# Attention into routed experts on one core: turned rows kept in DRAM, expert weights in pieces, and a written-out order for the last units' routing

## What is computed

```python
x = x + xattn(ctx, layernorm(x), mask)            # 64 x 128 tokens, 256 wide; 4 heads of 64
h = layernorm(x)
s = sigmoid(h @ router.T); f = s + router_bias    # 32 experts in 4 groups
# the 2 best groups by the sum of their 2 best f; then the 4 best experts of these
w = 2.5 * s[chosen] / sum(s[chosen])
y = sum_k w[k] * down[e_k] @ (silu(gate[e_k] @ h) * (up[e_k] @ h))
x = x + y + sdown @ (silu(sgate @ h) * (sup @ h)) # a shared expert, for every token
```

## Time and profile before

| | |
|---|---|
| median of three runs | 1495.28 us (1495.05 to 1497.76) |
| the profiled execution, its own time | 1499.18 us |
| its span, first to last instruction | 1497.4 us |
| mean granted TensorE clock | 0.978 of full speed |
| busy: PE, PEld, DVE, ACT, POOL | 90%, 70%, 64%, 71%, 41% |
| DMA | 241.80 MB, mean 161 GB/s |

### The profile page before, as it was taken

How to read it: one execution, slowest core, us unless ns; L and a number is a source line. 1 busy time by engine, 2 the same in 40 slices (tenths; PEclk the granted TensorE clock), 3 DMA queues, 4 the chain that set the end, 5 groups by cost and what they waited for, 6 DMA issues and landing times.

```text
span 1497.4 us, 33141 instructions
## 1 busy us (share of the span) xinstructions
PE 1347.0 (90%) x8742; PEld 1045.2 (70%) x8742; DVE 965.8 (64%) x4500; ACT 1057.4 (71%) x2886; POOL 610.7 (41%) x662
## 2 busy tenths in 40 slices
PE   3999999999999999997568888988988988889997
PEld 1566666666666666665457877877887887878886
DVE  3468888888888888887473444444444444437777
ACT  3899999999999999996534555555555555553432
POOL 1003444444544445445433555554555555540000
PEclk9899999999999999999699999999999999999999
DMA  7323454445444544443646444544544444419786
GB/s 227 123 81 137 175 175 141 153 173 174 153 144 168 177 174 136 157 149 132 190 134 228 139 142 144 144 141 133 145 141 139 146 143 138 115 42 341 275 287 206
DMA packets 145252, 241.80 MB, mean 161 GB/s; under 512 B 23467, under 2 KB 109357, under 8 KB 143792
## 3 DMA queue, kind: packets, MB, share of 16 engines
q1 hardware_dynamic: 118960, 172.27, 36.3%
q0 software_dynamic: 26112, 67.42, 12.6%
HBM read 102.20 MB, written 118.00 MB: 147 GB/s over the span
## 4 chain that ended last, share of the span: by engine, by line
PE 44%; ACT 34%; issue 10%; DVE 5%; another core or an unknown queue 3%; DMA 2%; POOL 1%; SPq 1%; ACTq 0%; DVEq 0%; POOLq 0%
PE psT L900 9%; PE psS L910 9%; PE ps L900 8%; ACT arena L1028 7%; ACT arena L1036 5%; PE ps L891 4%; PE ps L832 3%; ACT arena L1044 3%; PE psT L832 3%; ACT arena L996 2%; ACT arena L1000 2%; ACT arena L956 2%; PE psS L841 2%; ACT arena L988 1%
## 5 line engine op out<-in xcount | busy, mean ns | idle before, releaser
L588 POOL DMA_INDIRECT expert_out<-pay,dest x288 | 283.7, 985 | 269.5 <-DVE pay L1657 107.6
L533 POOL DMA_INDIRECT lists<-pay,slot x168 | 171.8, 1022 | 221.6 <-issue 49.2
L910 PE MATMUL psS<-arena,history 128*128 x576 | 182.2, 398 | 59.3 <-DVE history L1650 42.6
L1657 DVE TENSOR_SCALAR pay<-psS,dest 128x256 f32<-128x256 f32 x288 | 138.7, 481 | 77.3 <-PE psS L910 73.5
L900 PEld LDWEIGHTS ps<-pad 128*128 128x128 f32 x1152 | 149.5, 192 | 17.0 <-ACT pad L1196 7.9
L900 PEld LDWEIGHTS psT<-pad,hist_j 128*128 128x128 f32 x1152 | 150.4, 193 | 12.6 <-issue 2.2
L900 PE MATMUL ps<-pad 128*128 128x128 f32 x1152 | 154.0, 277 | 4.1 <-ACT pad L1196 2.6
L900 PE MATMUL psT<-pad,hist_j 128*128 128x128 f32 x1152 | 154.3, 277 | 0.9 <-ACT pad L1196 0.9
L910 PEld LDWEIGHTS psS<-arena,history 128*128 128x128 f32 x576 | 87.4, 192 | 76.7 <-issue 75.6
L533 POOL DMA_INDIRECT lists<-arena,slot x88 | 90.0, 1022 | 106.6 <-PE psT L711 19.7
L641 PE MATMUL ps<-arena 128*128 128x512 f32 x256 | 129.8, 630 | 1.9 <-ACT arena L988 1.7
(11 more groups left out here) (233 smaller groups left out, 3348.5 us busy)
## 6 DMA issues: line engine op xcount, KB each, us to landing
lists<-pad SPq DMA_DIRECT2D x72, 516.0 KB, 7.8
pay<-lists SPq DMA_DIRECT2D x288, 129.0 KB
arena<-expert_out SPq DMA_DIRECT2D x32, 1024.0 KB, 6.1
pay<-pay SPq DMA_DIRECT2D x40, 384.0 KB
x<-in_x SPq DMA_DIRECT2D x32, 256.0 KB
out<-arena SPq DMA_DIRECT2D x32, 256.0 KB, 4.9
arena<-arena SPq DMA_DIRECT2D x20, 384.0 KB
arena<-in_ctx SPq DMA_DIRECT2D x32, 192.0 KB
```

Source lines behind the costliest of these rows:

```text
L533: pool.indirect_dma_start(lists, bass.IndirectOffsetOnAxis(ap=slots(u)[:, j, k:k + 1], axis=0), paid(u)[:, j, k, :], None).then_inc(scat[u ...
L588: pool.indirect_dma_start(expert_out, bass.IndirectOffsetOnAxis(ap=dest[:, t % DESTS, 1:2], axis=0), yy[n], None, bounds_check=T * TOPK - ...
L910: pe.matmul(dbank[n % 2][:, 0:D], hh[:, n % 4, :], w_dn[:, at(e, 1), :].rearrange("p a n -> p (a n)"), start=True, stop=True)\
L1657: dve.tensor_scalar(yy[n], dbank[n % 2][:, 0:D], dest[:, t % DESTS, 0:1].bitcast(fp32), None, ALU.mult)\
```

## The change

A DRAM tensor `n1T_kept` takes the turned rows of units 0 to 7 while attention runs, and they are read back in step 31 into room that the last projections left. `EARLY` is 8. These eight units have no `norm_again`, no `shared_turn` and no `turned`; unit 0's `shared_up` stands inside attention's last step. Up's PSUM banks alternate by unit. Gate and up weights come from one DRAM tensor, in six DMAs: experts 0 to 5 and 14 to 16 after the last `turn_q`, 17 to 31 after the last output, then 6 to 8, 9 to 11 and 12 to 13 as the shared units have read their rows. Down weights 0 to 19 wait for the scatters of unit 28. Unit 30's copies are made by SP; unit 31's three copies by ACT, after its one row. Routing of units 29 to 31 is moved forward on PE, ACT and DVE and interleaved. The experts' two places for copied weights are swapped (not shown).

```diff
 EARLY = 7 -> 8;  IN_ARENA removed
+    n1T_kept = nc.dram_tensor("n1T_kept", [EARLY, P, 2 * D], fp32).ap()
+        early_n1T = arena[:, first_n1T * 2 * D:above * 2 * D].rearrange("p (u n) -> p u n", u=EARLY)
+        up_banks = [[ps[2], ps[0]], [ps[3], ps[1]]]
...
 SyncE
+            def save_n1T(u):
+                sp.wait_ge(e_n, u.n + 1)
+                sp.dma_start(n1T_kept[u.n], n1T.rearrange("p k n -> p (k n)")).then_inc(n1T_saved, 16)
+            def load_n1T():
+                sp.wait_ge(n1T_saved, 16 * EARLY)
+                sp.wait_ge(hats, UNITS)
+                sp.wait_ge(pb_full, NB)
+                sp.wait_ge(pc_full, NB)
+                sp.wait_ge(ss_done, NB)
+                for u in range(EARLY):
+                    sp.dma_start(early_n1T[:, u], n1T_kept[u]).then_inc(n1T_in[u], 16)
             def step(s):
                 if (s + 3).exists():
                     load(s + 3)
+                if s.n == UNITS - 1:
+                    load_n1T()
+                if (s + -2).exists():
+                    spread_rows(s + -2)
                 if s.exists():
                     blank_unit(s)
-                if (s + -2).exists() and s.exists():
-                    spread_rows(s + -2)
+                if (s + -2).exists() and s.n - 2 < EARLY:
+                    save_n1T(s + -2)
...
+            sp.wait_ge(t_q, UNITS)
+            load_experts(0, first_n1T)
+            load_experts(above, below_wo)
+            spread_rows(Unit(UNITS // 2 - 1, 0))
             sp.wait_ge(y_done, NB)
-            for k in range(2):
-                for which, w in ((0, gate), (1, up)):
-                    sp.dma_start(w_gu[:, :, k, which * I:(which + 1) * I], w[:, k]).then_inc(weights_e, 16)
-            sp.wait_ge(sx_done, 2 * IN_ARENA)
+            load_experts(below_wo, E)
+            sp.wait_ge(scat[1], scattered(1, UNITS - 1))
             sp.dma_start(w_dn[:, 0:early], down[:, 0:early]).then_inc(weights_e, 16)
+            for lo, hi in ((0, 3), (3, 6), (6, EARLY)):
+                sp.wait_ge(sgu_full, 2 * hi)
+                load_experts(first_n1T + lo, first_n1T + hi)
...
 TensorE, in step 31
                 if cc.exists():
                     logits(cc)
+                if not a.exists():
+                    shared_up(0, 0)
+                    shared_up(0, 1)
...
                 mix_values(s, 1)
+                else:
+                    positions(s + -2)
                 out_proj(s, 1)
...
 TensorE, behind it
+            turn_n1(last + -1)
+            shared_up(1, 0)
+            logits(last + -1)
+            shared_up(1, 1)
+            turn_n1(last)
+            logits(last)
+            positions(last + -1)
+            shared_down(0)
+            shared_up(2, 0)
+            shared_up(2, 1)
+            shared_down(1)
+            positions(last)
+            for u in range(3, EARLY):
+                shared_up(u, 0)
+                shared_up(u, 1)
+                if u == EARLY - 2:
+                    table_as_row()
+                shared_down(u - 1)
+            shared_down(EARLY - 1)
...
 in shared_up: waits
+                if u == 0 and mm == 0:
+                    pe.wait_ge(shared_in, 16 * 3)
+                    pe.wait_ge(lg_exp, UNITS - 2)
...
-                ge(pe, sh_done, 2 * u - 1 + mm)
+                ge(pe, sh_done, 2 * u - 3 + mm)
...
 ScalarE
             def n1_copy(u):
                 act.wait_ge(t_n, u.n + 1)
                 ge(act, lg_full, u.n)
+                ge(act, n1T_saved, 16 * upto(u.n, EARLY))
...
 ScalarE, in step 31 behind o_copy(s, 0)
+                if not a.exists():
+                    rows_to_scatter(s + -1, 0)
+                    rows_to_scatter(s + -1, 1)
...
 ScalarE, behind it
+            n1_copy(last + -1)
+            logit_exp(last + -1)
+            rows_to_scatter(last, 0)
+            rows_to_scatter(last, 1)
+            n1_copy(last)
+            logit_exp(last)
...
+                shared_silu(u, 0)
+                shared_silu(u, 1)
                 if u == 1:
+                    copy_rows(last, 0)
+                    copy_rows(last, 1)
...
 VectorE, in step 31: unit 28's slots ahead of invert_sums(s, 1); residual(31, 0) behind choose_experts
+                if not a.exists():
+                    weigh_and_give(r)
                 invert_sums(s, 1)
...
 VectorE, behind it
+            read_ranks(last + -2)
+            assign(last + -2, between_assigned)
             gather(last + 4)
+            norms(last + 4, between_last_roots)
             top_scores(last + -1)
             best_groups(last + -1)
             best_experts(last + -1)
             choose_experts(last + -1)
+            shared_hidden(0, 0)
+            shared_hidden(0, 1)
+            top_scores(last, between_last_choices)
+            best_groups(last, between_last_choices)
+            shared_hidden(1, 0)
+            shared_hidden(1, 1)
+            best_experts(last, between_last_choices)
+            code_part(last + -1, 1)
+            weigh_and_give(last + -1)
             choose_experts(last)
+            add_shared(0)
             read_ranks(last)
+            assign(last, between_last_needs)
+            assign_rest(last)
+            code_part(last, 0)
+            code_part(last, 1)
+            weigh_and_give(last)
+            add_shared(1)
...
```

More of the change, by code:

```diff
@@ L138, in build @@
         raw = part(2, 3 * D)
+        w_o = part(2, D)
         qT = part(2, 2, 2, P)
@@ L765, in positions, with shared_turn, shared_up, shared_down @@
                           start=True, stop=True).then_inc(pos_full, 1)
+            dbank = [psS[:, 0].rearrange("p a n -> p (a n)"), psS[:, 1].rearrange("p a n -> p (a n)")]
+            def shared_turn(u):
+                pe.wait_ge(nh, u - EARLY + 1)
+                ge(pe, nt_ev, u - EARLY)
+                for j in range(2):
+                    for k in range(2):
+                        m = pe.transpose(psO[:, k * D + j * P:k * D + (j + 1) * P],
+                                         n1_of(u)[:, j, k * P:(k + 1) * P], ident[:, :])
+                m.then_inc(nt_full, 1)
+            def shared_up(u, mm):
+                if u == 0 and mm == 0:
+                    pe.wait_ge(shared_in, 16 * 3)
+                    pe.wait_ge(lg_exp, UNITS - 2)
+                if u == 0 and mm == 1:
+                    pe.wait_ge(ranks_read, UNITS - 3)
+                if u == 1 and mm == 0:
+                    pe.wait_ge(pt_ev, NB)
+                if u == 1 and mm == 1:
+                    pe.wait_ge(y_done, NB)
+                if u < EARLY:
+                    pe.wait_ge(n1T_in[u], 16)
+                else:
+                    pe.wait_ge(nt_ev, u - EARLY + 1)
+                ge(pe, sh_done, 2 * u - 3 + mm)
+                for which, w in ((0, w_sg), (1, w_su)):
+                    for k in range(2):
+                        m = pe.matmul(up_banks[u % 2][mm][:, which * D:(which + 1) * D],
+                                      w[:, k, mm * P:(mm + 1) * P], n1T_of(u)[:, k, :], start=k == 0, stop=k == 1)
+                m.then_inc(sgu_full, 1)
+            def shared_down(u):
+                pe.wait_ge(sh_done, 2 * u + 2)
+                if u == 0:
+                    pe.wait_ge(pt_ev, NB - 1)
+                for j in range(2):
+                    ge(pe, sx_done, 2 * u + j - 1)
+                    for mm in range(2):
+                        m = pe.matmul(dbank[j][:, 0:D], gated(u)[:, mm, j * P:(j + 1) * P], w_sd[:, mm, :],
+                                      start=mm == 0, stop=mm == 1)
+                    m.then_inc(sd_full, 1)
             def step(s):
@@ new lines, in move_part @@
+            def move_part(u, k):
+                both = [P, 2, E]
+                dve.wait_ge(dS, S_LINKS * u.n + B_LINKS + k)
+                if k == 0:
+                    dve.tensor_tensor(delta[:, :, :], off_n[:, :, :], off[:, :, :], ALU.subtract).then_inc(dS, 1)
+                if k == 1:
+                    dve.tensor_tensor(later[:, :, :], later[:, :, :], delta[:, :, :].to_broadcast(both), ALU.mult)
+                    dve.scalar_tensor_tensor(moved[:, :, :], new[:, :, :], 0.0, delta[:, :, :], ALU.is_gt, ALU.mult)\
+                       .then_inc(dS, 1)
+                if k == 2:
+                    dve.tensor_tensor(code[:, :, :], code[:, :, :], later[:, :, :], ALU.add)
+                    dve.tensor_tensor(off[:, :, :], off[:, :, :], moved[:, :, :], ALU.add)
+                    dve.tensor_copy(kept[:, :, :], need[:, :, :])
+                    dve.tensor_copy(history[:, at(u.n, 1), :], given[:, u.par:u.par + 1, :]).then_inc(dS, 1)
@@ L1624, in _ @@
+            best_experts(last, between_last_choices)
+            code_part(last + -1, 1)
+            weigh_and_give(last + -1)
             choose_experts(last)
-            shared_step(3)
+            add_shared(0)
             read_ranks(last)
-            assign(last)
-            find_slots(last)
-            for q in range(NPT):
```

(13 more changed lines are left out.)

284 lines of the change are left out of this document (133 added, 151 removed).

## The result

The changed kernel takes 1484.78 us (median of nine runs, 1483.47 to 1491.26), against 1495.05 us for the kernel before in the same measurement: 10.3 us less, ratio 0.9941, 95% interval 0.9925 to 0.9957. The forecast was 24.3 us less. The profiled execution took 1483.47 us for a span of 1481.2. That is 15.7 us less than the 1499.18 us of the kernel before's profiled execution. So what follows accounts for some 16 us, and not for the 10.3 of the medians.

A forecast was written before the change was run, and what follows sets the result against it. PE was near full in attention, experts and late stage, so the question was the stretch from about 700 to 801 us. Net 18 us there plus 6.3 in the late stage made 24.3: 1471 us, range 1456 to 1486.

The forecast's parts named there:

- two rivals: Before the tiles: PE's clock falls in gaps, or VectorE's interleaving gains nothing and stalls return; 1480 each, chance 0.17 together.
- the residual near 728: End of attention: unit 31's last residual at 727.6 instead of 726.5, shared unit 0 costing about 1 us.
- no table load but one: Sign between attention and tiles: only one table load; two loads of 1.28 us ahead of units 30 and 31's exponentials gone.
- 24 late units at 5.62: Sign in the late stage: 24 shared units at 5.6 us each, one unit fewer than before.
- VectorE's serial sum: Routing after the residual: VectorE's work in series from 727.6 gives unit 31's slots at 755.4, against 779.3 before.
- PE: Between `positions(31)` at 749.1 and the tiles: five ups, six downs and the table's row take 28.7 us, ending at 777.8.
- PE becomes the bound: Before the tiles: PE's clock falls near 732 and 747, start at 790, time 1480; chance 0.17 shared with another rival.
- Saving and reading back: Attention: eight saves and eight loads of 256 KB cost 0, as waits have cover; upper end one 7.57 us landing.
- Weights: Before the tiles: last 0.5 MB piece, issued near 774.6, lands with the first tiles; cost 0, ends 0 and 7.5.
- Late stage: After the experts: one unit fewer, 5.62 us, and a looser bank wait, 0.7; 6.3 us gained, ends 3 and 8.
- Shared unit 0 in step 31: Attention's last step: unit 0's up products on the low clock delay the residual by about 1 us; ends 0 and 5.
- no stall: Step 31: ACT is not held, unit 0's up runs warm at 704.4, everything moves 9 us forward, 1462; chance 0.27.

The follow-up runs named there:

- e6: The changed kernel without an edit, run again beside the kernel before on another chip: 1381.12 us, ratio 0.9859 to the kernel before.
- e8: Changed kernel reading back only unit 0's turned rows in step 31, units 1 to 7 right ahead of the first weights piece: 1376.62 us, ratio 0.983.
- e13: The changed kernel without an edit, run once more in a later batch on another chip: 1380.35 us, ratio 0.9881 to the kernel before.
- e9: Changed kernel with units 1 to 7 read back after step 31 and add_shared(0) and add_shared(1) earlier in VectorE's order: 1370.73 us, ratio 0.9814.
- e10: Changed kernel with late read-back, early add_shared(0) and add_shared(1), and tiles ahead of the last gate and up weights piece: 1368.88 us, ratio 0.9788.
- e1: Changed kernel with add_shared(0) moved behind unit 1's products and add_shared(1) behind unit 31's choice in VectorE's order: 1375.24 us, ratio 0.984.
- e2: Changed kernel with SyncE issuing the first four pages and late down weights ahead of the last gate and up weights piece: 1374.41 us, ratio 0.9846.
- e3: Changed kernel with add_shared(0) and add_shared(1) earlier and the tiles ahead of the last gate and up weights piece: 1374.12 us, ratio 0.9843.
- e11: Changed kernel with units 1 to 7 read back after step 31 and tiles ahead of the last weights piece, additions unmoved: 1373.56 us, ratio 0.9823.
- e5: The kernel before without an edit, run for its trace on the follow-up chip: 1396.78 us, ratio 0.9985.
- e12: The kernel before with only the late stage's up products alternating banks by unit: 1393.23 us, ratio 0.9962.
- e7: Changed kernel with shared unit 0's up products moved out of attention's step 31 to right behind it: 1384.33 us, ratio 0.988.

## Why the prediction was wrong in size

The measured 1484.8 us lies inside the stated range, near its slow end, and near the 1480 of two rivals. That is in part luck: the wait that held TensorE is named in neither rival, and the late stage brought 3 us more than forecast.

**The account.** 24.3 us were forecast; the two traces differ by 16.2. Up to the tiles 18 were forecast, and 4.8 are left at the third tile; the experts and the late stage bring 2.1 and 3.0 more than forecast. The last 5.4 us down to 10.3 lie in where the profiled executions stand to their medians, which no trace can account for.

**Right.** The direction; the residual near 728 (729.8); no table load but one; 24 late units at 5.62; the 5.05 us before `logit_exp(29)` where I said some 6. VectorE's serial sum, from the residual to unit 31's slots, was 755.4 - 727.6 = 27.8 us: where no wait without a releaser lies in it, it measured 29.7 (e6), 28.0 (e8, e13) and 26.6 (e9, e10). In the first measurement it is 34.4.

**The step that failed** is *PE*: "Behind `positions(31)` at 749.1 stand five ups, six downs and the table's row: 28.7, so 777.8". The unit's price was good: in e10 the down products that follow 741.35 are 5.18 us apart. What I left out was a wait: `shared_down` needs the bank that `add_shared` frees, and I had myself placed `add_shared` behind the choice of unit 31 in VectorE's sum, without going back to see who waits for it on TensorE. It was 3.85 and 4.50 us, with matmuls at half speed after each: `positions(31)` came at 756.5 instead of 749.1, the chain's end at 792.8 instead of 777.8. Not all of these 15 us is the wait's. Unit 31's choice ended at 752.5 where I had 748.5, so VectorE itself was 4 us late: the residual 2.1, and two waits of 1.04 and 1.10 us without a known releaser on the way to the choice's end. The first wait for a bank ends with VectorE's additions right behind that choice, so part of it is VectorE's lateness; in e6, without unknown waits, the two are 2.16 and 2.12 us. e1 takes them away, and the stretch to the third tile is 6 us shorter; so 6 us is what is shown, and the rest of the 15 is read from the one trace. With the wait I would have had the rival "PE becomes the bound", 1480, for the forecast; its start of the experts at 790 is near what the trace shows (793.6), and two gaps of about its size with a fallen clock came, 13 to 17 us later than it put them.

***Saving and reading back*, "I take 0".** It was some 2.5 us by the traces, and more by the times (e8). I asked whether the transfers themselves are late, and they are not; what they delay is another transfer, the scatter for whose landing ScalarE waits before it reuses the rows' buffer. Between e6 and e8 these waits fall from 5.6 to 2.0 us in all. But e1, e2 and e3 have only one, of 2.3 to 3.0 us, and e9 to e11 one of 2.1 to 2.6 us, so these waits are not the whole of it. The cover named was the share of DMA in a mean step (0.37); the eight together are no mean.

***Weights*, "I take 0".** The order on SyncE's queue cost 0.5 us (e11 against e8) to 3 us (e2 against e6) in the traces, and a landing of 5.9 us after the last up product shows as soon as nothing else is late (e10). The forecast, "it lands with the first tiles", holds, but the tiles stood behind it: the third came 3.3 us late. I had counted to the first tile's turn and so missed this. To the third tile the gain of the whole turn is 4.8 us, not 18 (9.9 between e5 and e6).

**Late stage, 6.3.** 9.3 measured: 5.6 for the unit, as I had it, and 3.7 for the banks (e12) instead of 0.7. Waits of 0.49 us stood in the trace before, and I looked only at the repeated 5.62.

***Shared unit 0 in step 31*, "costs about 1 us".** Not shown: e7 has the residual within 1 us of e6. But the last steps of attention as a whole became 6 us longer in both measurements, which the prediction didn't have. 2.5 of it are the burst's, and taking unit 0 out doesn't shorten them (44.0 us in e7 against 43.8 in e6); what takes the rest is open.

**The rival "no stall".** In no trace of the four batches is there a wait without a releaser, and there the gain is 17 us, not the 33 that this rival had forecast; the wait for the banks, which the rival left out too, is part of what it lacks. By the trace, what the stalls add in the first measurement is not the same before and after: from the residual to the third tile the kernel before takes 78.6 us there and 77.4 in e5, the changed one 70.5 and 62.6. The prediction had drawn on the Trainium skill ("Runtime: NRT & Kernel Launch", Instruction fetch mechanics) that instruction fetch is mostly hidden in unrolled code. The later traces agree, as far as no wait without a known releaser is in them; the first measurement's 5.05 and 7.58 us do not, if they are fetch, and that no run shows.

**Open.** Where the waits without a known releaser come from, and whether they are what separates 10 us from 17. The traces don't show that distance in full: the spans differ by 16.2 us in the first measurement and by 18.2 between e5 and e6. Their return was tried for (e13) and they did not come; nothing here provokes them.

## What to carry to other kernels

When work is moved ahead on one engine, go through what it frees for the others: two banks freed late, by additions of 0.75 us each, held TensorE for 8 us, and the matmuls behind them ran at half the clock. Price a burst of DMAs by who waits for another landing at that time, not by the mean share. Compare stretches from an instant that lies ahead of the edit's first effect: the residual alone made the burst 4 us instead of 2.5. And count to the point at which the next stage runs at its steady rate, not to its first instruction.

## What the runs showed that I had not expected

The same kernel takes 1495 us in one measurement and 1397 to 1399 us on four chips, which agree within 0.2%. Nearly all of it is in the experts' 288 tiles, 1.87 against 1.56 us each at the same granted clock of 1.00 (windows above), though the waits without a releaser named there make only 30.6 us. They aren't the only ones: ScalarE also stands long where the profile names a product of TensorE. From 900 to 1200 us, in the first measurement and in e5:

```profile
ACT history L1207 <- PE psT L900: 44.9, 31, 2.9
```
```profile
ACT history L1207 <- PE psT L900: 46.1, 97, 0.5
```

There are a third as many such waits in the first, and they are up to 2.9 us long and not 0.5. In the first measurement one such wait, of 2.88 us, ends at 926.76, though the product that ScalarE then reads had ended at 924.3. So the sum of the unnamed waits is too low a price for whatever holds the engines there. A gain of 10 us found in the one surroundings was 17 in the other, so a change is best judged in both.

Two edits that each gain (behind the residual, e1 6 us and e2 3) gain together what the one does (e3). In e1 the third tile waits for a page that stands behind the last weights piece, and in e3 the first tile waits 2.20 us for that piece itself.
